# VectorE's loop of 267 instructions, and attention's probabilities signalled and turned token tile by token tile

## The chip, the cores and the metric

One core of a Trainium2 chip runs the whole program in one launch. The metric is the device time of that core in microseconds. The kernel before took 3623.44 us, the median of three runs (3611.81 to 3623.83).

## The reference, cut to what matters

The input is 64 blocks (graphs) of 256 tokens with 256 features, and for each block a 256 x 256 matrix `adj` of zeros and ones. All is float32. Four layers follow each other, each added to its input:

```
x = x + gnn0(layernorm(x), adj)     # graph attention: softmax over the edges, one head
x = x + mamba(layernorm(x))         # project, 4-tap causal convolution, silu, chunked state space, gate, project
x = x + gnn1(layernorm(x), adj)     # a weight matrix for each of 4 relations
x = x + moe(layernorm(x))           # 8 experts, one per token, capacity 1.25
```

The two parts that the change touches:

```
# the convolution, over time t, for each of 640 channels (5 blocks of 128)
conv[c, t] = conv_b[c] + sum(xBC[c, t - k] * conv_w[c, 3 - k] for k in range(4))
xBC = silu(conv)                    # 4 channel blocks are x, the fifth holds B and C
# the attention
e = where(adj > 0, leaky_relu(s1[:, None] + s2[None, :]), -9e15)
h = softmax(e, axis=-1) @ wh
```

## The kernel before, in words

A block's 256 tokens are two token tiles (T = 2) of 128 partitions. Each engine runs its own program, and the programs meet at semaphores only. The first three layers are a software pipeline: `step(b1, b2, b3, turn)` does the attention of block b1, the mamba layer of block b2 = b1 - 1 and the relations of block b3 = b2 - 1. `rounds` calls it: two opening steps and four more are written out, then comes a hardware loop (`eng.Fori`) of 28 iterations with two steps each, and then the closing steps. In the loop the count that a wait compares with is worked out by register instructions; in the unrolled steps it is a constant. Every second step (turn 0) holds `best_expert`, which picks each token's expert on VectorE, and `count` on TensorE; the other (turn 1) holds `slots`. Then 71 tiles of 256 tokens go through the experts; the change doesn't touch that part.

On VectorE a step is, in order: statistics of x (`deviation(0, ...)`, L828); `normalise(2, ...)` of x2 (L838); the taps of the convolution's block XB, which holds B and C; `remainder` (L909); the taps of the other four blocks; the chain of dt and the cumulative sums (L943 to L952); attention's leaky relu and masked maximum (L957, L962); xdt (L982); `slots` in turn 1; two products of the decay matrix with g (`weigh`, L855); with the sums of the exponentials done, x1 (L1007) and its statistics; two more products; y and its gating (L1023, L1028); row, the third residual (L1035); `best_expert` in turn 0; x2 (L1055) and its statistics; the logits lg (L1065).

Of the four taps ScalarE makes the first (`tap`, L628), and VectorE adds the other three in place (`taps`, L847). Each of these is followed by a wait of VectorE for its own instruction, since the next reads what it wrote. Three instructions of block XB, then three for each of the blocks 0 to 3: `conv_ready` goes up by 15 a step. TensorE waits for the third (it reuses bank 6 in L1289), ScalarE for the third and the fifteenth (the two silu).

In attention ScalarE makes the probabilities of each token tile (L726) and signals once after both. TensorE waits for that, turns the four 128 x 128 quarters into bank 0 (L1345), and signals; ScalarE copies them to `probT`, TensorE multiplies them with `wh` (L1370), and VectorE makes x1 from the result (L1007). When x1 is made, TensorE may fill banks 0 and 1 again with the next block's attention product (`attend`, L1181).

`need(eng, sem, n)` is a wait that is left out where n is a constant of zero or less. Many of them say that a buffer may be overwritten.

Of the kernel before, what the change touches and what calls it, by code (L numbers as in the profile page):

```python
# [5 lines left out]
ALU = mybir.AluOpType  # L6
ACT = mybir.ActivationFunctionType
# [13 lines left out]
def need(eng, sem, n):  # L21

    if isinstance(n, int) and n <= 0:
        return
    eng.wait_ge(sem, n)
# [24 lines left out]
def graph_mamba_moe(nc, io, out):  # L50
# [38 lines left out]
    with ctx:  # L89
# [531 lines left out]
        def _(act):  # L621
# [21 lines left out]
            def step(b1_, b2_, b3_, turn_):  # L643
# [51 lines left out]
                if b2_ is not None:  # L695
                    act.wait_ge(conv_ready, 15 * b2_ + 3)
                    need(act, g_made, b2_)
                    nc.scalar.activation(bT[:], conv[0:NS, XB, :], ACT.Silu)
                    nc.scalar.activation(cT[:], conv[NS:P, XB, :], ACT.Silu).then_inc(bc_ready, 1)
                    act.wait_ge(conv_ready, 15 * b2_ + 15)  # L700
                    need(act, yd_ready, 2 * b2_)
                    nc.scalar.activation(xs[:], conv[:, 0:XB, :], ACT.Silu).then_inc(xs_ready, 1)
                    act.wait_ge(proj_made, 5 * b2_ + 5)
                    nc.scalar.activation(zs[:, 2:4, :], bank[2][:, :], ACT.Silu).then_inc(zs_ready, 1)
# [17 lines left out]
                if b1_ is not None:  # L722
                    act.wait_ge(e_ready, b1_ + 1)
                    need(act, prob_turned, b1_)
                    for t in range(T):
                        ins = nc.scalar.activation(prob[:, t, :], e[:, t, :], ACT.Exp, bias=nmax[:, t:t + 1],  # L726
                                                   accum_out=esum[:, t:t + 1])
                    ins.then_inc(prob_ready, 1)
                    act.wait_ge(prob_turned, b1_ + 1)
                    need(act, hp_made, b1_)  # L730
                    copy(probT[:], bank[0][:, :]).then_inc(probT_ready, 1)
# [45 lines left out]
        def _(dve):  # L777
# [63 lines left out]

            def taps(c, b):

                src = bank[6][:, 0:N] if c == XB else bank[3 + c // 2][:, (c % 2) * N:(c % 2 + 1) * N]
                first = {XB: 0, 0: 3, 1: 6, 2: 9, 3: 12}[c]
                for k in range(1, TAPS):
                    v.scalar_tensor_tensor(conv[:, c, k:N], src[:, 0:N - k], conv_w[:, c, TAPS - 1 - k:TAPS - k],  # L847
                                           conv[:, c, k:N], ALU.mult, ALU.add).then_inc(conv_ready, 1)
                    dve.wait_ge(conv_ready, 15 * b + first + k)

# [60 lines left out]
            def step(b1_, b2_, b3_, turn_):  # L911
# [7 lines left out]
                if b2_ is not None:  # L919
                    if is_first(b2_):  # L920
                        dve.wait_ge(mix_in, 16 * len(mix_loads))
                    dve.wait_ge(tap_ready, 3 * b2_ + 1)
                    v.tensor_scalar(dt_pos[:], bank[6][:, N:2 * N], dt_b[:], 0.0, ALU.add, ALU.max)
                    taps(XB, b2_)
                if b3_ is not None:
                    remainder(b3_)
                if b2_ is not None:
                    for c in range(XB):
                        if c % 2 == 0:
                            dve.wait_ge(tap_ready, 3 * b2_ + 2 + c // 2)  # L930
                        taps(c, b2_)
                    if is_first(b2_):
                        dve.wait_ge(w_proj_made, 1)
                        for k in range(2):
                            ins = v.tensor_copy(w_proj[:, 2 * k:2 * k + 2, 0:D], bank[6 + k].rearrange("p (c d) -> p c d", d=D))
                        ins.then_inc(w_proj_ready, 1)
                        dve.wait_ge(a_exp, 1)
                        v.tensor_scalar(a_neg[:, 1:2], a_neg[:, 0:1], -1.0, None, ALU.mult).then_inc(a_ready, 1)
                        dve.wait_ge(a_ready, 1)

                    dve.wait_ge(dt_act, 3 * b2_ + 3)
                    need(dve, g_made, b2_)
                    ins = v.tensor_tensor(dt[:], dt_pos[:], dt_ln[:], ALU.add)  # L943
                    ins.then_inc(dt_ready, 1)
                    dve.wait_ge(dt_ready, b2_ + 1)
                    ch2.link(dve, v.tensor_scalar(dA[:], dt[:], a_neg[:, 1:2], None, ALU.mult), b2_)
                    ch2.link(dve, v.tensor_tensor_scan(cs[:], ones_row[:], dA[:], 0.0, ALU.mult, ALU.add), b2_)
                    ch2.link(dve, v.tensor_copy(cs_h[:], cs[:]), b2_)
                    ch2.link(dve, v.scalar_tensor_tensor(cs_r[:], cs_h[:], less_hi[:], cs[:], ALU.mult, ALU.add), b2_)
                    ch2.link(dve, v.tensor_copy(cs_m[:], cs_r[:]), b2_)  # L950
                    need(dve, expo_made, 8 * b2_)
                    v.scalar_tensor_tensor(cs3[:], cs_m[:], less_mid[:], cs_r[:], ALU.mult,  # L952
                                           ALU.add).then_inc(cs_ready, 1)
# [23 lines left out]
                if b2_ is not None:  # L977
                    dve.wait_ge(g_ready, b2_ + 1)
                    need(dve, y_made, 2 * b2_)
                    for t in range(T):  # L980
# [10 lines left out]
                if b1_ is not None:  # L991
                    dve.wait_ge(prob_ready, b1_ + 1)
                    ch1.link(dve, v.reciprocal(rsum[:], esum[:]), b1_)
# [20 lines left out]
                if b1_ is not None:  # L1014
                    need(dve, xn1_turned, b1_)
                    normalise(1, xn1, x1, xn1_ready, b1_)
                if b2_ is not None:
                    for u in range(2):
                        dve.wait_ge(y_made, 2 * b2_ + 1 + u)
                        if u == 0:  # L1020
                            need(dve, out_made, b2_)
                        for j in (2 * u, 2 * u + 1):
# [26 lines left out]
                if b2_ is not None:  # L1049
                    dve.wait_ge(rstd_ready[4], b2_ + 1)  # L1050
                    dve.wait_ge(x1b_ready, b2_ + 1)
                    if b3_ is not None:
                        dve.wait_ge(x2b_ready, b3_ + 1)
                    for t in range(T):
# [86 lines left out]
        def _(pe):  # L1141
# [90 lines left out]
            def step(b1_, b2_, b3_, turn_):  # L1232
# [36 lines left out]
                if b3_ is not None:  # L1269
                    if is_first(b3_):  # L1270
                        pe.wait_ge(rel_in, 16 * len(rel_loads))
                    if b2_ is not None:
                        pe.wait_ge(conv_ready, 15 * b2_ + 3)
                        pe.wait_ge(dt_act, 3 * b2_ + 1)
# [65 lines left out]
                if b1_ is not None:  # L1340
                    pe.wait_ge(prob_ready, b1_ + 1)
                    pe.wait_ge(wh_ready, b1_ + 1)
                    for k in range(T):
                        for t in range(T):
                            ins = turn(bank[0][:, k * N + t * P:k * N + (t + 1) * P], prob[:, t, k * P:(k + 1) * P],  # L1345
                                       identf[:])
                    ins.then_inc(prob_turned, 1)
# [163 lines left out]
```

## Time and profile before

| what | value |
|---|---|
| runs | 3623.83, 3611.81, 3623.44 us |
| the profiled execution | 3620.52 us |
| its span, first to last instruction | 3618.6 us |
| TensorE matmul busy | 3430.6 us (95%) |
| TensorE weight load busy | 2791.9 us (77%) |
| VectorE busy | 2565.8 us (71%) |
| GpSimd busy | 1784.1 us (49%) |
| ScalarE busy | 1734.8 us (48%) |
| mean granted TensorE clock | 0.981 |

The span is the time from the first to the last instruction of the execution that the profiler recorded. Register, branch, semaphore and DMA-issuing instructions don't count as busy. The pipelined steps take the first 2500 us or so of the span and the experts the rest; in the page's slices VectorE is busy for eight tenths and more in the former, and for four tenths in the latter.

### The profile page before, as it was taken

What the parts mean: (1) busy time and instruction counts of PE and PEld (TensorE: products, weight loads), DVE (VectorE), ACT (ScalarE), POOL (GpSimd) and SP (SyncE); (2) the same over time, 40 slices, a digit from 0 to 9 for tenths busy, and PEclk for the clock granted to TensorE, in tenths of its full rate; (3) what the DMA queues carried; (4) which work ended last, traced back from release to release, by engine and by line L of the source; (5) the groups of instructions that cost most, each with busy time, mean ns of one, the idle gap of its engine ahead of it and who ended that gap; (6) DMA issues with size and microseconds to landing.
All of it is one profiled execution on the core that took longest, in us unless ns stands there. A gap on an engine that the chain in (4) does not pass through costs nothing.

```text
span 3618.6 us, 63010 instructions
## 1 busy us (share of the span) xinstructions
PE 3430.6 (95%) x19338; PEld 2791.9 (77%) x19338; DVE 2565.8 (71%) x7349; ACT 1734.8 (48%) x3690; POOL 1784.1 (49%) x2043
## 2 busy tenths in 40 slices
PE   7999999999999999999999999999599999999998
PEld 6777777777777777777777777777488888888887
DVE  4888887888888788888888888888344444444444
ACT  3655655655555555565555566565133232232332
POOL 2455454554444455445555554555355455455553
PEclk8999999999999999999999999999799999999999
DMA  3111111111111111111111111110255555555553
GB/s 120 39 36 51 38 36 50 39 36 48 41 36 36 50 39 36 41 47 36 47 42 36 41 47 36 44 45 25 90 199 190 194 200 190 192 199 193 191 200 128
DMA packets 168301, 305.78 MB, mean 85 GB/s; under 512 B 38000, under 2 KB 140400, under 8 KB 149936
## 3 DMA queue, kind: packets, MB, share of 16 engines
q0 software_dynamic: 38272, 196.98, 15.7%
q1 hardware_dynamic: 92880, 72.41, 6.9%
q10 hardware_dynamic: 36960, 34.62, 3.3%
q14 instruction: 162, 1.33, 0.1%
q8 instruction: 27, 0.44, 0.1%
HBM read 250.77 MB, written 53.17 MB: 84 GB/s over the span
## 4 chain that ended last, share of the span: by engine, by line
PE 77%; DVE 12%; issue 6%; POOL 1%; ACT 1%; another core or an unknown queue 1%; DMA 0%; DVEq 0%; ACTq 0%; SPq 0%; POOLq 0%
PE bank L1444 13%; PE bank L1458 13%; PE bank L1188 9%; PE bank L1172 8%; PE bank L1403 6%; PE bank L1289 6%; PE bank L1388 5%; DVE conv L847 4%; PE bank L1181 3%; PE bank L1370 3%; PE bank L1320 1%; DVE decay L855 1%; DVE stats L828 1%; PE bank L1345 1%; PE bank L1216 1%
## 5 line engine op out<-in xcount | busy, mean ns | idle before, releaser
L768 ACT ACTIVATE decay<-bank,w_up 128x256 f32<-128x256 f32 x568 | 269.0, 474 | 700.8 <-PE bank L1444 693.0
L1172 PE MATMUL bank<-xn1T,w_in 128*128 128x256 f32 x2304 | 523.8, 381 | 5.7 <-issue 4.5
L1188 PE MATMUL bank<-w_rel,hT 128*128 128x264 f32 x2048 | 523.4, 394 | 0.0
L1444 PE MATMUL bank<-zs,w_up 128*128 128x256 f32 x2272 | 504.5, 380 | 0.6 <-ACT zs L623 0.6
L1458 PE MATMUL bank<-w_dn,decay 128*128 128x256 f32 x2272 | 502.1, 379 | 0.0
L847 DVE SCALAR_TENSOR_TENSOR conv<-bank,conv_w,conv 128x255 f32<-128x255 f32 (+2 forms) x960 | 461.4, 481 | 34.6
L1172 PEld LDWEIGHTS bank<-xn1T,w_in 128*128 128x128 f32 x2304 | 432.5, 190 | 64.5 <-issue 8.2
L1444 PEld LDWEIGHTS bank<-zs,w_up 128*128 128x128 f32 x2272 | 433.4, 191 | 60.3 <-issue 0.9
L1458 PEld LDWEIGHTS bank<-w_dn,decay 128*128 128x128 f32 x2272 | 426.2, 190 | 55.1
L1120 DVE TENSOR_TENSOR hT<-bank,w_dn 128x256 f32<-128x256 f32 x142 | 60.3, 425 | 536.8 <-PE bank L1458 536.8
L1188 PEld LDWEIGHTS bank<-w_rel,hT 128*128 128x128 f32 x2048 | 364.0, 190 | 79.3 <-issue 20.7
L482 POOL TENSOR_TENSOR rstd<-ve,mhalf 128x2 f32<-128x2 f32 x256 | 218.2, 853 | 389.3 <-DVE ve L833 344.3
L496 POOL TENSOR_SCALAR masks<-adjt_sb 128x512 fp32r<-128x512 int32 x256 | 404.3, 1592 | 5.4
L1289 PE MATMUL bank<-masks,xp 128*128 128x512 f32 x1024 | 287.9, 429 | 66.3 <-DVE conv L847 57.9
L855 DVE TENSOR_TENSOR decay<-decay,g 128x768 f32<-128x768 f32 x256 | 253.1, 1029 | 92.8 <-ACT decay L737 86.1
L361 POOL TENSOR_TENSOR beats<-mhalf 128x1 f32<-128x1 f32 x372 | 80.3, 216 | 462.6 <-DVE hT L1120 336.0
L1289 PEld LDWEIGHTS bank<-masks,xp 128*128 128x128 f32 x1024 | 197.4, 201 | 142.1 <-issue 67.9
L533 POOL TENSOR_TENSOR x2b<-x,b_rel 128x264 f32<-128x264 f32 x128 | 92.9, 746 | 417.1 <-DVE xdt L982 406.3
L737 ACT ACTIVATE decay<-bank 128x384 f32<-128x384 f32 x512 | 209.8, 496 | 124.0 <-PE bank L1226 90.3
L1403 PE MATMUL bank<-w_proj,y 128*128 128x264 f32 x1024 | 240.4, 387 | 3.1 <-DVE y L1028 3.0
L623 ACT ACTIVATE xn1T<-bank 128x512 f32<-128x512 f32 x64 | 38.2, 597 | 391.2 <-PE bank L1167 391.2
L1403 PEld LDWEIGHTS bank<-w_proj,y 128*128 128x128 f32 x1024 | 188.8, 190 | 35.5 <-DVE y L1028 6.5
(238 smaller groups left out, 6167.5 us busy)
## 6 DMA issues: line engine op xcount, KB each, us to landing
token_rows<-row SPq DMA_DIRECT2D x64, 266.0 KB, 2.9
xT_sb<-in_xT ACTq DMA_DIRECT2D x64, 256.0 KB
x_sb<-in_x ACTq DMA_DIRECT2D x64, 256.0 KB, 3.0
adj_sb<-in_adj SPq DMA_DIRECT2D x64, 256.0 KB, 3.2
adjt_sb<-in_adjT SPq DMA_DIRECT2D x64, 256.0 KB, 3.4
out<-row SPq DMA_DIRECT2D x64, 256.0 KB, 2.4
w_in<-token_rows,idc POOLq DMA_INDIRECT x142
out<-hT,ids POOLq DMA_INDIRECT x142
```

The lines of the kernel that those rows point to most:

```text
L482: gp.tensor_tensor(rstd[i][:], ve[i][:], mhalf[:], ALU.pow).then_inc(rstd_ready[i], 1)
L496: ins = gp.tensor_scalar(masks[:, :, r, :], adjt[:], float(r + 1), None, ALU.is_equal)
L737: nc.scalar.activation(decay[:, h, :], bank[EXPO[h % 4]][:, 0:TRI], ACT.Exp).then_inc(decay_ready, 1)
L768: nc.scalar.activation(hid(f), bank[f % 4][:, 0:GROUP], ACT.Relu, bias=b1[q % 2][:, f:f + 1]).then_inc(hid_ready, 1)
L847: v.scalar_tensor_tensor(conv[:, c, k:N], src[:, 0:N - k], conv_w[:, c, TAPS - 1 - k:TAPS - k], conv[:, c, k:N], ALU.mult, ALU.add).then_i ...
L855: v.tensor_tensor(decay[:, 2 * j:2 * j + 2, :], decay[:, 2 * j:2 * j + 2, :], g[:, 0:TRI].unsqueeze(1).broadcast_to([P, 2, TRI]), ALU.mult ...
L1172: ins = mm(dst, w_in[:, k, first:first + P], xn1T[:, k, :], start=k == 0, stop=k == DK - 1)
L1188: ins = mm(bank[6 + t][:, 0:GX], hT[:, d, r * N + t * P:r * N + (t + 1) * P], w_rel[:, r, d, :], start=r == 0 and d == 0, stop=r == R - 1 ...
L1289: ins = mm(bank[6 + c][:, :], xp[part][:, t, d * P:(d + 1) * P], masks[:, t, 2 * c:2 * c + 2, :], start=t == 0 and part == 0, stop=t == T ...
L1403: ins = mm(bank[(4, 2)[t]][:, 0:GX], y[:, j, t * P:(t + 1) * P], w_proj[:, j, :], start=j == 0, stop=j == XB - 1)
L1444: ins = mm(bank[f % 4][:, 0:GROUP], w1[i][:, k, f * P:(f + 1) * P], xgT[:, k, :], start=k == 0, stop=k == DK - 1)
L1458: ins = mm(bank[4 + j][:, 0:D], hid(f)[:, j * P:(j + 1) * P], w2[i][:, f, :], start=f == 0, stop=f == FB - 1)
```

## The change

`taps` takes a tuple of blocks. For each of the taps 1 to 3 it issues one instruction for each block of the tuple, and only the last of them signals and is waited for. It is called for (XB,), then for (0, 1) and for (2, 3), so `conv_ready` goes up by 9 a step; all that wait for it count by 9. Five `need` waits of VectorE are gone (for g_made, expo_made, y_made, xn1_turned and out_made), and before x2 so is the wait for x2b_ready, and the one for x1b_ready except in the last such step. ScalarE signals `prob_ready` after each token tile's probabilities. TensorE waits for tile 0, turns its two quarters, waits for tile 1, and turns its two; VectorE waits for both as before.

```diff
             # ScalarE
-                    act.wait_ge(conv_ready, 15 * b2_ + 3)
+                    act.wait_ge(conv_ready, 9 * b2_ + 3)
...
-                    act.wait_ge(conv_ready, 15 * b2_ + 15)
+                    act.wait_ge(conv_ready, 9 * b2_ + 9)
...
                     for t in range(T):
-                        ins = nc.scalar.activation(prob[:, t, :], e[:, t, :], ACT.Exp, bias=nmax[:, t:t + 1],
-                                                   accum_out=esum[:, t:t + 1])
-                    ins.then_inc(prob_ready, 1)
+                        nc.scalar.activation(prob[:, t, :], e[:, t, :], ACT.Exp, bias=nmax[:, t:t + 1],
+                                             accum_out=esum[:, t:t + 1]).then_inc(prob_ready, 1)
             # VectorE
-            def taps(c, b):
-
-                src = bank[6][:, 0:N] if c == XB else bank[3 + c // 2][:, (c % 2) * N:(c % 2 + 1) * N]
-                first = {XB: 0, 0: 3, 1: 6, 2: 9, 3: 12}[c]
+            def taps(blocks, b):
+
+                first = {XB: 0, 0: 3, 2: 6}[blocks[0]]
                 for k in range(1, TAPS):
-                    v.scalar_tensor_tensor(conv[:, c, k:N], src[:, 0:N - k], conv_w[:, c, TAPS - 1 - k:TAPS - k],
-                                           conv[:, c, k:N], ALU.mult, ALU.add).then_inc(conv_ready, 1)
-                    dve.wait_ge(conv_ready, 15 * b + first + k)
+                    for c in blocks:
+                        src = bank[6][:, 0:N] if c == XB else bank[3 + c // 2][:, (c % 2) * N:(c % 2 + 1) * N]
+                        ins = v.scalar_tensor_tensor(conv[:, c, k:N], src[:, 0:N - k], conv_w[:, c, TAPS - 1 - k:TAPS - k],
+                                                     conv[:, c, k:N], ALU.mult, ALU.add)
+                    ins.then_inc(conv_ready, 1)
+                    dve.wait_ge(conv_ready, 9 * b + first + k)
...
-                    taps(XB, b2_)
+                    taps((XB,), b2_)
...
-                    for c in range(XB):
-                        if c % 2 == 0:
-                            dve.wait_ge(tap_ready, 3 * b2_ + 2 + c // 2)
-                        taps(c, b2_)
+                    for u in range(2):
+                        dve.wait_ge(tap_ready, 3 * b2_ + 2 + u)
+                        taps((2 * u, 2 * u + 1), b2_)
...
-                    need(dve, g_made, b2_)
...
-                    need(dve, expo_made, 8 * b2_)
...
-                need(dve, y_made, 2 * b2_)
...
-                    dve.wait_ge(prob_ready, b1_ + 1)
+                    dve.wait_ge(prob_ready, 2 * b1_ + 2)
...
-                    need(dve, xn1_turned, b1_)
...
-                        if u == 0:
-                            need(dve, out_made, b2_)
...
-                    dve.wait_ge(x1b_ready, b2_ + 1)
-                    if b3_ is not None:
-                        dve.wait_ge(x2b_ready, b3_ + 1)
+                    if b1_ is None:
+                        dve.wait_ge(x1b_ready, b2_ + 1)
             # TensorE
-                        pe.wait_ge(conv_ready, 15 * b2_ + 3)
+                        pe.wait_ge(conv_ready, 9 * b2_ + 3)
...
-                    pe.wait_ge(prob_ready, b1_ + 1)
                     pe.wait_ge(wh_ready, b1_ + 1)
-                    for k in range(T):
-                        for t in range(T):
+                    for t in range(T):
+                        pe.wait_ge(prob_ready, 2 * b1_ + t + 1)
+                        for k in range(T):
                             ins = turn(bank[0][:, k * N + t * P:k * N + (t + 1) * P], prob[:, t, k * P:(k + 1) * P],
                                        identf[:])
                     ins.then_inc(prob_turned, 1)
```

The loop body of VectorE's compiled program has 300 instructions before the change, register, semaphore and branch instructions counted.

## Rows read from the trace of the kernel before

**Rows 1.** The page: busy time and instructions of each engine.
```profile
PE 3430.6 (95%) x19338; PEld 2791.9 (77%) x19338; DVE 2565.8 (71%) x7349; ACT 1734.8 (48%) x3690; POOL 1784.1 (49%) x2043
```
**Rows 2.** Windows, first two steps, then 53: length, busy (instructions), clock, DMA share, GB/s.
```profile
859.20:899.30 40.10, 37.25 (x229) 28.98 (x229) 31.21 (x90) 22.31 (x47) 21.63 (x23) 1.00 0.14 40
899.30:936.60 37.30, 36.67 (x226) 28.86 (x223) 34.01 (x103) 22.09 (x46) 18.23 (x20) 1.00 0.14 43
312.90:2390.20 2077.30, 1975.50 (x11928) 1549.79 (x11929) 1728.54 (x5030) 1178.12 (x2465) 1051.41 (x1141) 0.99 0.14 41
```
**Rows 3.** Waits, 312.9 to 2390.2 us: who waited for whom, us in total, times, longest.
```profile
PE bank L1289 <- DVE conv L847: 57.9, 27, 2.6
PE bank L1181 <- DVE x L1007: 15.8, 29, 3.0
PE bank L1345 <- ACT prob L726: 8.1, 15, 0.6
PE bank L1172 <- issue: 4.5, 24, 0.3
...
DVE stats L828 <- issue: 100.3, 27, 4.2
DVE x L1055 <- POOL rstd L482: 21.7, 27, 0.8
```
**Rows 4.** Timeline, step with the branch: start, us, engine line, ..., [idle before <- releaser].
```profile
862.06 0.36 DVE L1065 SCALAR_TENSOR_TENSOR lg<-row,gate_b 128x8 f32<-128x8 f32 x2
866.13 0.75 DVE L828 BATCH_NORM_STATS2 stats<-x_sb 128x6 f32<-128x256 f32 x2 [3.72 <-issue]
...
870.21 2.10 PE L1289 MATMUL bank<-masks,xp 128*128 128x512 f32 x8 [2.13 <-DVE conv L847]
...
883.02 0.66 PE L1345 MATMUL bank<-identf,prob 128*128 128x128 f32 x4 [0.50 <-ACT prob L726]
...
855.87 0.45 ACTq L646 DMA_DIRECT2D x_sb<-in_x  x1
```
**Rows 5.** Timeline of the other step, VectorE, TensorE and ScalarE.
```profile
907.54 6.25 DVE L847 SCALAR_TENSOR_TENSOR conv<-bank,conv_w,conv 128x255 f32<-128x255 f32 x12
...
922.54 2.28 DVE L855 TENSOR_TENSOR decay<-decay,g 128x768 f32<-128x768 f32 x2
...
924.92 0.89 DVE L1007 SCALAR_TENSOR_TENSOR x<-bank,rsum,x_sb 128x264 f32<-128x264 f32 x2
...
929.71 0.86 DVE L1023 SCALAR_TENSOR_TENSOR y<-xs,d_col,bank 128x256 f32<-128x256 f32 x2
...
925.96 2.09 PE L1181 MATMUL bank<-w_gc,xT_sb 128*128 128x274 f32 x8 [0.45 <-DVE x L1007]
...
921.60 1.64 ACT L737 ACTIVATE decay<-bank 128x384 f32<-128x384 f32 x4 [0.27 <-PE bank L1226]
```
**Rows 6.** The page's DMA queues: kind, packets, MB, share of 16 engines.
```profile
q14 instruction: 162, 1.33, 0.1%
```
**Rows 7.** The same of one iteration, 862.5 to 939.8 us.
```profile
q14 instruction: 5, 0.04, 0.2%
```
**Rows 8.** The same of 864.0 to 864.6 and of 933.0 to 933.8 us.
```profile
q14 instruction: 1, 0.01, 3.2%
...
q14 instruction: 1, 0.01, 4.0%
```
**Rows 9.** Windows of two unrolled or first-pass steps and of two long ones.
```profile
196.80:233.60 36.80, 36.42 (x227) 28.75 (x223) 33.84 (x102) 22.08 (x46) 18.04 (x20) 1.00 0.15 44
233.60:275.40 41.80, 38.20 (x230) 30.06 (x230) 31.07 (x91) 22.22 (x47) 21.40 (x24) 0.96 0.14 39
936.60:980.80 44.20, 39.48 (x229) 29.83 (x229) 31.48 (x92) 22.31 (x47) 21.10 (x23) 0.96 0.13 37
1097.20:1142.90 45.70, 39.99 (x229) 30.55 (x229) 31.28 (x91) 22.30 (x47) 22.03 (x23) 0.93 0.13 35
```
**Rows 10.** Timeline of ScalarE in the longest of them.
```profile
1128.48 1.64 ACT L737 ACTIVATE decay<-bank 128x384 f32<-128x384 f32 x4 [4.30 <-remote]
```

## The prediction

> **What bounds the kernel now.** The page's first part comes first: TensorE is busy for 95% of the span, VectorE for 71%, so TensorE sets the time, and only idle TensorE can be won [rows 1]. Next the windows by step. A step is the time from one block's first projection to the next block's. The hardware loop holds two steps: the first one after the branch back ("after-branch step") took 40.1 us, the second 37.3 us [rows 2]. In the former TensorE is busy 37.25 us, in the latter 36.67 us. The unrolled step at 196.8 us, of the same work as the latter, took 36.8 us [rows 9]. The window from 312.9 to 2390.2 us holds 27 after-branch steps and 26 others: 2077.3 - 26 x 37.3 = 1107.5 us, 41.0 us for each after-branch step.
>
> Then TensorE's waits in that window [rows 3]: 57.9 us for the depthwise convolution (L1289 behind VectorE's L847), 27 times, thus once an iteration; 15.8 us for x1 (L1181 behind L1007); 8.1 us for the probabilities (L1345 behind ScalarE's L726). VectorE's own largest is not a wait for anybody: 100.3 us of "issue", 27 times, at the first instruction after the branch. The timeline shows one: VectorE's last instruction starts at 862.06 and ends at 862.42, the next starts at 866.13, though its input was long there. TensorE is then 2.13 us late at L1289 and 0.50 us at L1345 [rows 4]. ScalarE's branch back costs nothing: its x_sb load is issued at 855.87, between two squares [rows 4]. In the other step VectorE has no gap up to x1, and TensorE waits 0.45 us for it at L1181 [rows 5].
>
> **Why the branch is slow.** The DMA queues name instruction transfers: q14, 162 packets in 1.33 MB, so 8.2 KB each [rows 6]. One iteration has five [rows 7], and single windows place them at 864.0-864.6, 866.5-867.1, 870.5-871.1, 901.5-902.2 and 933.0-933.8 us, one each ([rows 8] has the first and the last of the five). Compiled, VectorE's loop of the kernel before is 300 instructions, ScalarE's 180, TensorE's 957. Counting VectorE's instructions against these times: about 128 lie between the last three transfers. My reading: a block holds some 128 instructions, and entering a block fetches the next. The body begins 18 instructions (give or take 4) before the end of a block, so it lies in four blocks (18 + 128 + 128 + 26). Entering the fourth fetches a fifth, the first is gone, and the branch must fetch it (the packet inside the 3.72 us gap), then the second and third. ScalarE's 180 lie in two blocks by the same count, and none of the five transfers is left over for it. A buffer of two blocks would miss there and one of five would hit on VectorE, so it keeps three or four.
>
> **The change, part by part.**
> *The loop's length.* 267 instructions instead of 300. In three blocks (384) they fit if they begin at most 117 into a block. They begin 110 into one now, and the unrolled steps before the loop only lose instructions (waits on constants), so the start moves to between about 80 and 110. With four blocks kept, the first is still there at the branch: the 3.72 us go 27 times. VectorE's own gain is 100 us; TensorE's is read from its steps. Taking 2.13 and 0.50 out of 40.1 leaves 37.5 us [rows 2, 4]; TensorE is busy for 37.25 of them, and the rest is short waits for what the late VectorE made, so I take 37.3. The conv of the first block would be ready 3.7 us sooner, and TensorE needed it only 2.13 us sooner: 1.6 us of slack. From 41.0 to 37.3, 27 times: 100 us.
>
> This includes an irregular part. The two longest after-branch steps took 44.2 and 45.7 us with the clock granted at 0.96 and 0.93 [rows 9]; in the latter ScalarE's exponentials start 4.30 us late, put down to nobody [rows 10]. The first pass of the loop, with no branch before it, has such a step too (41.8 us, clock 0.96) [rows 9]. Beyond 40.1 us the two hold 4.1 + 5.6 = 9.7 us. The cause isn't visible. I let half go with the idle time and put back 5 us.
>
> *Taps by two blocks.* Each tap waits for the one before. Twelve such in a row took 6.25 us, (6.25 - 0.48) / 11 = 0.52 us from one start to the next; two independent ones of the same kind and size (L1023) take 0.86 us together, so the second starts 0.39 us after the first [rows 5]. Six pairs a step lose one dependence each: 6 x 0.13 = 0.8 us of VectorE per step. The removed waits were for things long done; between dependent instructions they show as short gaps, and I count 0.1 us. The other side of this bound: if a pair's second instruction gained nothing, 0; if every removed wait were a whole one, 1.2 us. I take 0.8, since L1023 is the same operation reading the same kind of bank.
> What lies on the path: in the other step x1 comes at 924.92 after two decay products that end at 924.82. They can't start before ScalarE's exponentials (921.60 plus 1.64, so 923.24), which leaves at most 923.24 + 0.95 + 0.15 = 924.3 for x1: 0.6 us to win [rows 5]. TensorE needs 0.45. The wait goes, with little to spare: 26 x 0.45 = 12 us in the window, and some 3 us in the seven steps before and behind it at up to the same 0.45. If VectorE gained nothing here, 0. What is late next is TensorE itself: VectorE's later idle time grows.
>
> *Convolution and silu.* ScalarE's silu of xs waits for the last tap as before, now 0.8 us sooner; it is off the path in the second step. The first blocks of a pair finish later than they did, but nobody waits for them singly.
>
> *Removed waits* (g_made, expo_made, y_made, xn1_turned, out_made, x2b_ready, x1b_ready): each is covered by a wait that stays, so nothing starts earlier by them; they count as loop length.
>
> *Probabilities by token tile.* TensorE turns tile 0 while ScalarE makes tile 1. One wait is added on TensorE, with the turn of tile 1 and everything after it behind it, and one register operation; such waits show as 4.5 us in 24 places at L1172 (0.19 us each) where TensorE has run dry, and as nothing under full queues [rows 3]. In the second step L1345 has no wait at all, so 0. In the after-branch step part of the 0.50 us, two turns of 0.66 / 4 = 0.16 us each, would go by this alone [rows 4]; with the stall gone it has no worth of its own. I bound it by -0.3 and +0.1 us a step, and take 0. VectorE waits for count 2b+2, the same moment as before.
>
> **The sum.** 3620.5 (the profiled execution, 1.9 us around a span of 3618.6) - 100 - 15 + 5 = 3510.5 us. That execution lies 2.9 us under the median of the runs, 3623.44, and 8.7 above the lowest. I forecast 3510 us.
> Its own range: the steps may keep 0.3 us of what I take out (56 x 0.3 = 17) or the pauses all stay (+8): 3535; all go and the register waits shrink too: 3494.
>
> **The rivals.**
> *The stall stays.* For: the trace shows only that a body in four blocks misses and one in two doesn't; 267 lies in three. If the buffer keeps three blocks, entering the third fetches the fourth and drops the first. Then 2.13 us remain, and the gain is the probabilities' 8.1 us, 12 + 3 us at L1181 and little else: 3620.5 - 23 = 3597 us. Against: four is the rounder size, and the count excludes only five and more. Chance 0.14.
> The Trainium skill ("Runtime: NRT & Kernel Launch", Instruction fetch mechanics) says the same in a stronger form: the buffer of an engine other than TensorE is two pages of 256 instructions, and a taken branch to a target outside them stalls. By that rule 267, more than a page, would still stall, and the time would be that 3597. The trace disagrees in the size: 8.2 KB packets in [rows 6], half of the page's 16 KiB; where it is right in the total of 512 instructions, it speaks for four blocks of 128.
> *Half of it.* The stall goes, but the after-branch step finds another limit at 38.5 us (best_expert adds VectorE work late in it, and TensorE's count waits for it): 27 x 1.2 = 32 us less gain, 3543 us. For: VectorE waits there 27 times, up to 0.8 us, for GpSimd's rstd before it can make x2 [rows 3], so the end of this step is a chain through three engines. Against: the same chain ends the step now, and TensorE's busy time of 37.25 us has no room for it [rows 2]. Chance 0.07.
> *Slower.* With fewer rests TensorE pauses more often, as in the 45.7 us step (5.6 us over the common one, clock 0.93 [rows 9]). From 110 / 5 = 22 more such pauses the gain is used up; at 27 the time is 3510 + 27 x 5 = 3645 us. For: one happened without a stall before it. Against: the second step, the denser one, takes 37.3 us each time. Chance 0.03.
>
> **Chances.** Forecast 0.76, stall stays 0.14, half 0.07, slower 0.03. The range that holds 8 in 10 has to reach the stall's case: 3494 to 3600 us; the likeliest case alone 3494 to 3535. About 0.5% (18 us) is what a measurement can tell from no change. Faster by more than that: 0.76 + 0.07, and of the stall's 0.14, as 3597 is only 0.6% below 3620, some 0.06: 0.89. Within 0.5%: 0.07. Slower: 0.04.
>
> **What would show it.** Right: VectorE's "issue" at L828 gone, q14 down from 162 packets to about 30, TensorE's waits at L1289 for L847 gone, both steps at 36.9 to 37.3 us, starts of paired taps 0.39 us apart. Wrong: 27 gaps of 3.7 us still there, steps of 40 us; or the wait at L1289 gone and a new one behind it.

## The result and the profile after

The changed kernel takes 3515.0 us, the median of four runs (3513.94 to 3518.75); the kernel before, on the same chip, 3621.56 us (3611.81 to 3623.83). The ratio is 0.971, with a 95% interval of 0.969 to 0.973. The forecast was 3510 us.

The page's first part, busy time and instructions of each engine, against [rows 1]: the engines run the same numbers of instructions, and TensorE is busy for 97% of a shorter span.
```profile
PE 3396.7 (97%) x19338; PEld 2783.3 (79%) x19338; DVE 2532.4 (72%) x7349; ACT 1723.9 (49%) x3690; POOL 1788.3 (51%) x2043
```
The instruction queue on the page, against [rows 6] (kind, packets, MB, share): five packets an iteration are gone.
```profile
q14 instruction: 27, 0.22, 0.0%
```
The same windows as in [rows 2] (first two steps of one iteration, then the 53 steps of the loop), and two long steps, which answer to [rows 9]. Columns: length, busy us of TensorE, its weight loads, VectorE, ScalarE and GpSimd, granted clock, DMA share, GB/s.
```profile
834.00:870.70 36.70, 36.63 (x228) 29.14 (x229) 30.62 (x89) 22.08 (x47) 21.52 (x23) 1.00 0.16 43
870.70:907.80 37.10, 36.47 (x228) 28.96 (x225) 33.58 (x103) 21.98 (x46) 18.25 (x20) 1.00 0.13 42
308.30:2285.20 1976.90, 1944.07 (x11928) 1542.89 (x11929) 1701.22 (x5029) 1167.79 (x2465) 1055.31 (x1141) 1.00 0.15 43
752.80:797.00 44.20, 39.31 (x229) 30.73 (x229) 30.63 (x89) 22.08 (x47) 21.08 (x23) 0.92 0.14 36
984.10:1025.10 41.00, 38.33 (x229) 30.03 (x229) 30.68 (x89) 22.08 (x47) 21.91 (x23) 0.96 0.15 39
```
The spans differ by 3618.6 - 3513.2 = 105.4 us. The loop's window has 2077.3 - 1976.9 = 100.4 of them, the steps before it 312.9 - 308.3 = 4.6, what follows it 0.4. The gain lies in the loop.

TensorE's waits in the loop's window, against [rows 3]:
```profile
PE bank L1174 <- DVE x L1004: 17.5, 31, 2.7
PE bank L1381 <- ACT decay L736: 7.5, 3, 4.8
PE bank L1165 <- issue: 5.9, 24, 0.3
```
The 57.9 us for the convolution have no successor at L1282 (L1289 before), and the 8.1 us for the probabilities none at L1338. The wait for x1 (L1174, before L1181) is still there: 17.5 us, where 15.8 were. VectorE's waits in the same window: 100.3 us of "issue" are gone, and nothing of its size has come.
```profile
DVE decay L856 <- ACT decay L736: 69.9, 28, 4.9
DVE xdt L979 <- ACT g L623: 39.9, 53, 1.0
DVE ve L1039 <- PE bank L1403: 38.3, 26, 1.5
...
DVE x L1048 <- POOL rstd L482: 21.7, 27, 0.8
```
VectorE's timeline at the branch, against [rows 4]: the first statistics of the next iteration start 0.42 us after the last instruction of the one before started. It was 4.07 us, 3.72 of them idle.
```profile
836.88 0.35 DVE L1058 SCALAR_TENSOR_TENSOR lg<-row,gate_b 128x8 f32<-128x8 f32 x2
837.30 0.75 DVE L827 BATCH_NORM_STATS2 stats<-x_sb 128x6 f32<-128x256 f32 x2
```
The timeline of the other step, against [rows 5] (ScalarE's g and exponentials, VectorE's three, TensorE's that waits, and GpSimd's masks, which will matter):
```profile
889.41 0.50 ACT L623 ACTIVATE g<-bank 128x400 f32<-128x400 f32 x1
...
889.95 1.29 DVE L979 TENSOR_TENSOR xdt<-bank,g 128x512 f32<-128x512 f32 x2 [0.50 <-ACT g L623]
...
892.78 1.64 ACT L736 ACTIVATE decay<-bank 128x384 f32<-128x384 f32 x4 [0.27 <-PE bank L1219]
...
893.05 4.41 POOL L496 TENSOR_SCALAR masks<-adjt_sb 128x512 fp32r<-128x512 int32 x3
...
893.68 2.26 DVE L856 TENSOR_TENSOR decay<-decay,g 128x768 f32<-128x768 f32 x2
...
896.05 0.89 DVE L1004 SCALAR_TENSOR_TENSOR x<-bank,rsum,x_sb 128x264 f32<-128x264 f32 x2
...
897.09 2.09 PE L1174 MATMUL bank<-w_gc,xT_sb 128*128 128x274 f32 x8 [0.40 <-DVE x L1004]
```
Read step by step over the whole loop (from one first projection to the next):

| | before | after | saved |
|---|---|---|---|
| after-branch step, median | 40.50 | 36.66 | |
| the same, mean of 27 | 41.00 | 37.52 | 3.48 x 27 = 94 us |
| other step, median | 37.30 | 37.09 | |
| the same, mean | 37.3 | 37.07 | 0.25 x 26 = 6 us |

The mean after the branch stands above the median because of seven long steps, such as the 44.2 and 41.0 us above: together they take 23 us more than common ones. With the first pass of the loop, which has one too (40.5 us, 41.8 before), it is eight and 27 us. I call such a step's excess over the median a pause; below, the pauses of a kernel are counted with the first pass, from 0.5 us of excess on.

Where the time of a pause goes can be read. In the 44.2 us step ScalarE stands before the second four of its exponentials, and TensorE then waits for them at L1381:
```profile
783.92 1.64 ACT L736 ACTIVATE decay<-bank 128x384 f32<-128x384 f32 x4 [7.40 <-remote]
785.69 5.39 PE L1381 MATMUL bank<-decay,xdt 128*64 128x256 f32 x32 [4.84 <-ACT decay L736]
```
In a common step the same ScalarE gap is 1.22 us (859.00) and the same 32 products take 2.82 us (862.05). TensorE's clock is granted at 1.2 GHz and not 2.4 from 784.3 us, when the engine had been idle since 780.9, to 791.1 us. So the step pays twice: 4.84 us of idle time and 2.57 us of slower products, of 7.5. In seven of the eight long steps ScalarE stands for 2.4 us or more before one of its two fours of exponentials. "remote" means that no instruction in the trace is the releaser: the products that ScalarE waits for end at 777.7, but their four semaphore updates are recorded at 783.90 to 784.00 us. In the common step they end at 858.97 and the updates stand at 858.98 to 859.08.

One number of the prediction has to be corrected first. Compiled, VectorE's loop body of the changed kernel is 279 instructions, not 267: the change's 267 leaves out 12 memsets that the count of 300 for the kernel before includes. The unrolled steps ahead of the loop lose 18. So by the prediction's own reading (blocks of 128, the body of the kernel before starting at place 110) the new body starts at 110 - 18 = 92 and ends at 92 + 279 = 371, still within three blocks (384).

### The profile page after: what moved, and what is told of

Its sections match the earlier page's. It is cut to its first block, busy times and chain, and to the rows that moved or that the text cites. A ratio compares the mean times of both kernels' runs of the same rounds, so it can differ in the third digit from the quotient of the medians.

```text
span 3513.2 us, 62394 instructions
## 1 busy us (share of the span) xinstructions
PE 3396.7 (97%) x19338; PEld 2783.3 (79%) x19338; DVE 2532.4 (72%) x7349; ACT 1723.9 (49%) x3690; POOL 1788.3 (51%) x2043
## 4 chain that ended last, share of the span: by engine, by line
PE 91%; issue 3%; DVE 3%; ACT 1%; POOL 1%; another core or an unknown queue 1%; DMA 1%; ACTq 0%; DVEq 0%; SPq 0%; POOLq 0%
PE bank L1165 14%; PE bank L1437 14%; PE bank L1451 14%; PE bank L1181 12%; PE bank L1282 7%; PE bank L1396 6%; PE bank L1381 5%; PE bank L1174 4%; PE bank L1363 3%; PE bank L1313 2%; PE bank L1235 2%; PE bank L1304 1%; DVE x L1004 1%; PE bank L1209 1%; PE bank L1403 1%
## 5 line engine op out<-in xcount | busy, mean ns | idle before, releaser
L1181 PE MATMUL bank<-w_rel,hT 128*128 128x264 f32 x2048 | 523.5, 394 | 0.0
L847 DVE SCALAR_TENSOR_TENSOR conv<-bank,conv_w,conv 128x255 f32<-128x255 f32 (+2 forms) x960 | 425.9, 477 | 20.8
L1181 PEld LDWEIGHTS bank<-w_rel,hT 128*128 128x128 f32 x2048 | 364.0, 190 | 80.0 <-issue 24.2
L856 DVE TENSOR_TENSOR decay<-decay,g 128x768 f32<-128x768 f32 x256 | 251.2, 1022 | 95.1 <-ACT decay L736 90.2
L1282 PE MATMUL bank<-masks,xp 128*128 128x512 f32 x1024 | 275.5, 413 | 5.7 <-ACT xp L623 5.6
L1282 PEld LDWEIGHTS bank<-masks,xp 128*128 128x128 f32 x1024 | 188.5, 189 | 68.6 <-ACT hT L623 25.7
```

The lines of the kernel that those rows point to most:

```text
L847: ins = v.scalar_tensor_tensor(conv[:, c, k:N], src[:, 0:N - k], conv_w[:, c, TAPS - 1 - k:TAPS - k], conv[:, c, k:N], ALU.mult, ALU.add)
L856: v.tensor_tensor(decay[:, 2 * j:2 * j + 2, :], decay[:, 2 * j:2 * j + 2, :], g[:, 0:TRI].unsqueeze(1).broadcast_to([P, 2, TRI]), ALU.mult ...
L1181: ins = mm(bank[6 + t][:, 0:GX], hT[:, d, r * N + t * P:r * N + (t + 1) * P], w_rel[:, r, d, :], start=r == 0 and d == 0, stop=r == R - 1 ...
L1282: ins = mm(bank[6 + c][:, :], xp[part][:, t, d * P:(d + 1) * P], masks[:, t, 2 * c:2 * c + 2, :], start=t == 0 and part == 0, stop=t == T ...
```

## The experiments

**Theory A** (the prediction's): the branch stalls when VectorE's body reaches into four blocks of some 128 instructions; position and length decide together. **Rival B**: the removed waits and pairs themselves made the loop fast. **Rival C**: only the body's length decides (300 too long, 279 not). The first four kernels tell them apart. They shift the body by cheap one-column memsets that run once, ahead of VectorE's first step:

**1. The kernel before, shifted by 30.**
```
+ spare = sb("spare", [P, 30])
+ for i in range(30):
+     v.memset(spare[:, i:i + 1], 0.0)
```
The body keeps its 300 instructions and all its waits; it starts at 110 + 30 - 128 = 12 and ends at 312.

> The kernel before, with nothing changed but 30 one-column memsets on VectorE ahead of its first step (some 2 us, beside the first loads). The loop body stays 300 instructions; its start moves from about the 110th place of a 128-instruction block to about the 12th, so it lies in three blocks (12 + 300 = 312, under 384) and not four. Theory A (position: the branch misses when the body touches four blocks): the 27 gaps of 3.7 us at L828 go, q14 falls from 162 packets to under 40, time about 3525 us, nearly all of the change's gain. Theory B (length: fewer instructions, or fewer waits, are what helped): the gaps stay, 3620 us.

Measured: 3541.66 us against 3633.77 of the kernel before beside it, ratio 0.975 (0.973 to 0.977). The page's instruction queue:
```profile
q14 instruction: 27, 0.22, 0.0%
```
Thirty added instructions, none in the loop, take (3633.77 - 3541.66) / 27 = 3.4 us off each iteration. B and C both fall: no wait was removed and the length is the same. Its steps are 36.77 and 37.30 us (medians), with thirteen long ones that hold 43.5 us. The time is 17 us over the expected 3525; the kernel before took 12 us more on this chip, too, than in the comparison above.

**2. The changed kernel, shifted by 30.** The same edit on the changed kernel: 279 instructions from place 122 to 401, in four blocks.

> The changed kernel with the same 30 memsets ahead of the first step. The body is the changed one (279 instructions in the compiled program), but starts near place 122, and 122 + 279 = 401 is over 384: four blocks. Theory A: the stall comes back whole, 27 gaps of 3.7 us, over 150 q14 packets, about 3600 us. Theory B: no gap, 3515 us plus at most 2.

Measured: 3666.54 us, ratio 1.009 (1.007 to 1.011): slower than the kernel before, with every part of the change in it. The page, then the waits of its loop, then VectorE at one branch:
```profile
q14 instruction: 162, 1.33, 0.1%
```
```profile
DVE stats L828 <- issue: 107.7, 27, 4.4
...
PE bank L1285 <- DVE conv L848: 96.6, 27, 4.0
...
DVE xn L838 <- issue: 30.5, 27, 1.3
```
```profile
1039.34 0.36 DVE L1059 SCALAR_TENSOR_TENSOR lg<-row,gate_b 128x8 f32<-128x8 f32 x2
1043.56 0.75 DVE L828 BATCH_NORM_STATS2 stats<-x_sb 128x6 f32<-128x256 f32 x2 [3.87 <-issue]
...
1045.91 0.73 DVE L838 TENSOR_SCALAR xn<-x,mv,rstd 128x256 f32<-128x256 f32 x2 [1.11 <-issue]
```
The stall is back, with the 162 packets, to the number those of [rows 6]. What the expectation of some 3600 us missed is the second gap: the body runs through a few instructions and enters the next block, whose transfer isn't there yet, and VectorE stands for another 1.11 us. Counted in the trace with register and semaphore instructions, nine instructions of the body come before this gap, not the 6 of place 122: the body starts at about 119. The kernel before then starts at 119 - 12 = 107, and the 21 instructions up to its block's end covered the transfer (it has no such gap). So TensorE waits 96.6 us for the convolution instead of 57.9. Its clock is granted at 0.96 or less in each of the 27 after-branch steps, and in about half of them in the kernel before (mean of the execution 0.973, against 0.981), which is part of why the step takes 41.95 us (median).

**3. The changed kernel, shifted by 60** (places 24 to 303), a control for the memsets.

> The changed kernel with 60 memsets ahead, the control for the one with 30: the body starts near place 24 of the next block, 24 + 279 = 303, three blocks again. Theory A: no gap, about 3515 us, though more memsets were added than in the slow one. If the memsets themselves cost something, over 3520 us here and less with 30.

Measured: 3525.88 us, ratio 0.971 (0.969 to 0.973), steps 36.67 and 37.09 us, 27 packets. The memsets cost nothing that shows; the place decides.

**4. The removed waits alone.** Taps one by one and probabilities as before:
```
- need(dve, g_made, b2_)
- need(dve, expo_made, 8 * b2_)
- need(dve, y_made, 2 * b2_)
- need(dve, xn1_turned, b1_)
- need(dve, out_made, b2_)
...
+ if b1_ is None:
      dve.wait_ge(x1b_ready, b2_ + 1)
```
291 instructions; the unrolled steps lose the same 18, so 92 to 383 by the prediction's count: one place short of the fourth block.

> The kernel before with only the seven waits of a step removed. Compiled, the body falls from 300 to 291 instructions and the unrolled part before it loses 18, so it starts near place 92 and ends at 383 of 384, with my uncertainty of 4 places. Theory A: either no stall at all (about 3525 us) or the whole stall (about 3618 us), nothing between. Theory B (gain in proportion to the instructions removed, 9 of 21): about 3575 us.

Measured: 3530.37 us, ratio 0.972 (0.970 to 0.974), steps 36.74 and 37.31 us.
```profile
q14 instruction: 27, 0.22, 0.0%
```
A few removed waits that nobody waited for give nearly the whole gain, by moving and shortening the code.

**5 and 6. The edge: shifted by 16 and by 8.** Places 108 to 387 and 100 to 379.

> The changed kernel with 16 memsets ahead of the first step: the body of 279 starts near place 108 and ends near 387, just over three blocks of 128. Theory A (three blocks fit, four don't, and the block's size is 128): the stall is back, over 150 q14 packets, 27 gaps at L828. If the capacity is something else (as a total of 400 or more), no stall.

> The same with 8 memsets: start near place 100, end near 379, inside three blocks. Theory A: no stall, under 40 q14 packets. Together with the run with 16 it places the edge between them, within the 4 places by which my start is uncertain.

Measured, one run each: 3511.58 and 3513.4 us, 27 packets in both. The shift by 8 is as expected. The one by 16 isn't: by my places it reached 3 into the fourth block. The second gap of experiment 2 says why. It puts every start some 3 places lower, which is within the 4 that the prediction allowed, and so this body at 105 to 384, just inside three blocks. The packets agree: in experiment 2 the last three of an iteration start when VectorE has begun the 15th, 138th and 262nd instruction of its body, in the kernel before the 26th, 150th and 281st, in all 27 iterations to within one. Moved by 18 - 16 = 2 places, the last would stand at the 283rd, and this body has 279. That a block holds some 128 instructions rests on these distances (123 to 131) and on the 8.2 KB packets [rows 7, 8]; it is not measured to the instruction. One rival is hardly touched by the shifts: that only the place of the start decides, whatever the length. It would need its limit between this start and that of the kernel before, 2 places higher.

**7 and 8. The other two parts, each alone, with the stall out of the way** (both on the shifted kernel of experiment 1). Taps by two blocks (`for c in blocks:` inside the tap loop, one signal for each pair), and the probabilities tile by tile:
```
- for k in range(T):
-     for t in range(T):
+ for t in range(T):
+     pe.wait_ge(prob_ready, 2 * b1_ + t + 1)
+     for k in range(T):
```


> The kernel before with its loop shifted by 30 memsets (no stall) and the taps paired, nothing else. Without the pairing the common steps took 36.77 us after the branch and 37.30 us for the second; in the changed kernel 36.66 and 37.09. If the pairing is what separates them: 36.7 and 37.1 here. If it is the removed waits or the split of the probabilities: 36.77 and 37.30.

> The kernel before with its loop shifted by 30 memsets (no stall) and the probabilities signalled and turned tile by tile, nothing else. My forecast was 0 for this part once the stall is gone: 36.8 and 37.3 us, as without it. Rival: the added wait costs up to 0.1 us a step, or the earlier turn of tile 0 gains up to 0.3 us a step.

Measured, one run each: 3502.57 us with the taps, steps 36.77 and 37.06 us; 3518.42 us with the probabilities, steps 36.67 and 37.37 us. Against 36.77 and 37.30 of experiment 1, pairing gives 0.24 us in the other step and nothing after the branch, so 28 x 0.24 = 7 us; the probabilities -0.10 and +0.07, nothing. The totals mislead here: the first is 39 us under experiment 1, but its pauses hold 9.7 us where the other's held 43.5, a difference of 34. The two also ran on different chips, on which the kernel before took 3615.74 and 3633.77 us. I don't take 3502.57 for a faster version: by its common steps it is the changed kernel (36.66 and 37.09).

**9. What holds up x1.** In the changed kernel VectorE waits 0.50 us for g (889.41, behind ScalarE's load of the table for Exp). Theory G: g ahead of that load brings x1 earlier by up to 0.4 us. Rival: the exponentials and probabilities then come later by as much.
```
- nc.scalar.preload_act_table(ACT.Exp)
  (the copy of g)
+ nc.scalar.preload_act_table(ACT.Exp)
```


> The changed kernel, with ScalarE's copy of g moved ahead of the load of the exponential's table (one statement moved, same instructions). In the changed kernel VectorE waits 0.5 to 1.0 us in each step at xdt (L979) for g, 46.8 us in all, and TensorE still waits 0.40 us for x1 at L1174 in each second step. Theory G (VectorE's gain from the paired taps is lost in this wait): xdt starts about 0.5 us sooner, the 0.40 us at L1174 go, second steps fall from 37.09 to about 36.7 us, time down by about 28 x 0.4 = 11 us or 0.3% against the changed kernel (ratio to before about 0.968). Rival: ScalarE's probabilities come 0.5 us later and TensorE waits at its turn of them instead: no gain or a loss of a few us.

Measured: 3536.93 us, ratio 0.979 (0.977 to 0.980), so slower than the changed kernel (0.971) by 0.8%, more than the few us of the rival; steps 37.43 and 37.38 us. Windows of two steps, the two waits of the whole execution that grew, and the timeline behind the exponentials:
```profile
842.40:879.90 37.50, 36.92 (x229) 29.09 (x229) 31.16 (x90) 22.19 (x47) 21.88 (x23) 1.00 0.15 43
879.90:917.30 37.40, 36.66 (x227) 28.84 (x224) 33.58 (x103) 22.09 (x46) 18.96 (x20) 1.00 0.14 42
```
```profile
PE bank L1174 <- DVE x L1004: 28.2, 59, 2.4
DVE decay L856 <- ACT decay L736: 133.5, 65, 4.0
```
```profile
901.65 5.11 POOL L496 TENSOR_SCALAR masks<-adjt_sb 128x512 fp32r<-128x512 int32 x3
...
903.12 2.29 DVE L856 TENSOR_TENSOR decay<-decay,g 128x768 f32<-128x768 f32 x2 [0.78 <-ACT decay L736]
```
G falls. VectorE's wait moved from g to the exponentials (133.5 us in place of 90.2 in the whole execution of the changed kernel), and TensorE now waits for x1 in both steps (59 times in place of 40, 28.2 us in place of 22.1). The idle time before xdt was not the limit; the exponentials behind it were.

**10. Where the pauses come from.** They fall in steps of the after-branch kind alone (the first of an iteration's two), which also hold GpSimd's scatter of slot numbers, four indirect DMAs that it issues 12.1 to 16.1 us into the step. Theory P: the scatter makes them. Theory Q: something else of that step. The edit moves the scatter to the end of the other step (`to_place` returns `turn_[0] - 1` in turn 1).

> The changed kernel, with GpSimd's scatter of slot numbers (four indirect DMAs for each group) moved from the first kind of step (after the branch) to the end of the second kind. The irregular pauses of 1 to 8 us lie in the first kind alone, in every run so far (27 us in all in the changed kernel). Theory P (the scatter makes them): they move into second steps, or go. Theory Q (something else of the first kind, as best_expert, or the loop's iteration): they stay in the first kind, in about the same iterations (profile steps 5, 19, 23 to 31).

Measured: 3641.82 us, ratio 1.007 (1.006 to 1.009); steps 41.50 and 37.05 us. The waits of its loop:
```profile
DVE x L1047 <- POOL rstd L482: 156.6, 27, 5.8
```
```profile
PE bank L1164 <- DVE x L1047: 81.8, 27, 3.1
```
The scatter stands ahead of the rstd that x2 needs, and the whole of it comes onto the path: a wait of 0.8 us at most in the changed kernel is 5.8 here. Four steps are still long (42.7 to 43.4 us, 6.3 us of excess in all, where 17 to 27 were), and they are after-branch steps. But the scatter hasn't left these: it runs across the start of the step, here one that starts at 785.3 us.
```profile
784.71 1.09 POOL L489 DMA_INDIRECT slot_ids<-tid,slot  x1 [0.15 <-issue]
786.11 0.97 POOL L489 DMA_INDIRECT slot_ids<-tid,slot  x1 [0.31 <-issue]
```
The pauses' own gap is gone: in the loop's window ScalarE has no wait of "remote" at its exponentials, where the changed kernel had 24.1 us in six. What is left of that kind is earlier in the step, as the scatter is, and short:
```profile
ACT z L708 <- remote: 1.9, 1, 1.9
ACT hT L622 <- remote: 1.7, 1, 1.7
```
So the place and size of the pauses changed with the scatter's place, which speaks for P. It isn't shown: the new wait of 5.8 us leaves the rest of the step more room, and the other edit that would tell, a kernel without the scatter, wasn't run.

**11. The slow product.** The second of the two decay products takes 1.38 us where the first takes 0.96 (893.68 and 894.56 in the changed kernel). One of GpSimd's masks starts at 894.53. In the kernel of experiment 9 it is the first product, at 903.12, that takes 1.42 us, and there a mask starts at 903.13. One more one-column product on GpSimd ahead of the masks should shift them against VectorE's.
```
+ carry(pool)
  edge_masks(0, R - 1)
```


> The changed kernel with one more one-column product on GpSimd (0.19 us) ahead of its edge masks in each step. In every run so far the second decay product of the second kind of step takes 1.38 to 1.41 us where the others take 0.95 us; it starts 0.03 us after GpSimd has begun its second mask. In the first kind it starts before the first mask ends, takes 0.95 us, and the mask takes 2.2 us and not 1.5. Theory C (the two engines take turns, and the later one waits, so that 0.15 us of order decide 0.43 us of VectorE): with the masks 0.19 us later the product takes 0.95 us in both kinds, the mask 2.2 us, TensorE's 0.40 us at L1174 go, second steps 37.09 -> 36.7 us, and the time falls by 28 x 0.4 = 11 us against after_again. Rival D (the 1.38 us come from what the product reads or from ScalarE): products and steps as before, 0 us.

Measured: 3513.28 us, ratio 0.970 (0.969 to 0.972), steps 36.76 and 37.25 us.
```profile
899.03 4.40 POOL L496 TENSOR_SCALAR masks<-adjt_sb 128x512 fp32r<-128x512 int32 x3
...
899.65 2.28 DVE L857 TENSOR_TENSOR decay<-decay,g 128x768 f32<-128x768 f32 x2
```
The products begin 0.62 us behind the masks here and 0.63 us in the changed kernel (893.05 and 893.68): both moved together, so the order that I wanted to change stayed, and the second product still takes 1.41 us. The experiment missed its aim. Over the whole of the changed kernel, 29 of the 256 products start within 0.05 us of a mask's start, and all 29 take 1.37 to 1.39 us; the first product above, which starts 0.63 us into a mask, takes 0.96. That the common start is the cause is argued, not shown.

**12. The changed kernel again, without an edit,** to see how much pauses vary.

> The changed kernel, unchanged: its ratio on this chip, for comparison with after_beat, and a second profile of it. The irregular pauses: if they belong to the loop's iterations (the data or the program), the same profile steps are long as before (5, 13, 19, 23, 25, 27, 29, 37); if they are chance, other ones are.

Measured: 3510.5 us, ratio 0.970 (0.969 to 0.972), steps 36.68 and 37.08 us. Counted from the kernel's first step as 0, so that the loop's window begins with step 7, its long steps are 5, 13, 19, 25, 27 and 29, and they hold 17 us. In the first profile it was the same six with 23 and 37 (11 just passes 0.5 us), and 27 us. Step 5 is long in all other kernels but that of experiment 10, step 19 in all but the one with the taps of experiment 7; the other numbers come and go. So pauses are no pure chance: some iterations have them nearly always, and their sum varies by ten microseconds and more between executions. Over all kernels here they held 6 to 43 us of a profile. Differences between kernels under some 20 us must be read from the common steps, not from one total.

## Why the prediction was right

**The stall.** Right in mechanism, shown by experiments 1 to 4 in both directions: it can be taken out of the unchanged loop and put into the changed one by its place alone. The reading of the packets (five an iteration, blocks of some 128, four kept) gave both signs. The rule of the Trainium skill ("Runtime: NRT & Kernel Launch", Instruction fetch mechanics) that I weighed as a rival is two pages of 256 instructions and a stall for a target outside them. What these runs exclude is my reading of it, by which any body longer than a page stalls: 300 instructions in a row are taken back without a stall in experiment 1, and 279 stall in experiment 2. The stalls alone don't exclude its page size: of all kernels here, the two that touch four blocks of 128 are also the only ones that would touch three pages of 256, if such pages ended at places 128 and 384. What speaks for 128 is the packets, 8.2 KB each and some 128 instructions apart. The rule's total of 512 instructions agrees with four blocks of 128.

**The count of 267** was wrong (279), and the conclusion held since 371 is still under 384. Had the unrolled steps not lost 18 instructions, it would not have held: 110 + 279 = 389. The prediction should have tried both counts.

**The size of the after-branch step.** Predicted 37.3 us, measured 36.66: 27 x 0.64 = 17 us more than forecast. The step at fault was taking TensorE's busy 37.25 us [rows 2] for a floor: in the same step it is busy 36.63 us now, with the same products. Part of the difference is how busy time adds up. In the changed kernel the first mask product starts at 842.60 us, 0.35 us before the projection's last one ends (835.88 + 7.07 = 842.95), and the two overlap; in the kernel before the projection ended at 868.08 and TensorE stood still, with nothing to overlap. So a wait that goes takes some busy time with it.

**The pauses.** I put back 5 us; the window has 23 in seven steps: 18 us less gain. They need no stall before them. That half of them would go with the idle time was a guess, and a wrong one. I called the cause not visible; the row that I had shows the place at least, since its 4.30 us [rows 10] are the same ScalarE gap as the 7.40 us above. The wrong guess cancels the error before it: 94 us saved after the branch where 95 were forecast. So the forecast's closeness here is partly luck.

**Pairing and x1.** Each pair did gain: the starts of the taps from 991.83 to 993.13 us lie 0.40, 0.50 and 0.40 apart, thus 0.90 us for a pair and a dependence where two single taps took 1.03, 0.8 us in six pairs, as forecast. What failed is the ceiling behind it. I allowed 0.95 us for what follows the exponentials to x1; the second product takes 1.38, and the row that I worked from had it (two products in 2.28 us, so 1.14 each on average [rows 5]). With it, x1 at 923.24 + 1.38 + 0.15 = 924.77 leaves 0.15 us to win and not 0.6. Measured, x1 comes 25.62 - 25.35 = 0.27 us sooner in its step. The wait went from 0.45 to 0.40 us, not to zero. The step still gained 0.21 to 0.24 us, so 6 us with a few outside the loop, where 15 were forecast.

**The probabilities.** Predicted nothing within -0.3 and +0.1 us a step; measured -0.10 and +0.07, in one run.

**The sum** with the measured terms: 3620.5 - 27 x (41.00 - 36.66) + 23 (pauses) - 6 (other step) - 5 (outside the window) = 3515 us, which is the profiled execution's time; it must be, since its terms are taken from that profile. The rivals "stall stays" and "half" are excluded by the 27 packets and by 36.66 us; "slower" had a true part, since pauses without a stall are there, but it needed 110 us of them, and 23 are there.

**Open:** why the semaphore updates that ScalarE waits for come up to 6.2 us late, whether the scatter does it, and why some iterations have it nearly always; the edge of a block to the instruction; whether the mask's start lengthens the product.

## What to carry to other kernels

Where an engine's first instruction after a loop's branch waits for "issue" and the instruction queue moves packets every iteration, count the loop's compiled instructions and where they start in their blocks: moving the loop, by a few instructions ahead of it, can be worth more than shortening it, and an edit that does nothing else can lose it again. When two versions are compared, compare common steps first and count the long ones apart; a total mixes them. Before earlier work is credited with time, follow the chain behind it to its next input, with the duration that an operation has in that place, not its shortest.

## What the runs showed of the hardware

VectorE's instruction fetch here moves 8.2 KB a packet, and a body that reaches into four blocks of some 128 instructions costs 3.7 to 3.9 us at each branch, while one of the same length in three costs nothing that shows. A body that started some nine instructions before a block's end paid a second time, 1.11 us; one that started some 21 before it did not. The same VectorE product took 0.95 us, or 1.37 to 1.42 us when a GpSimd instruction began at the same moment. TensorE's semaphore updates were recorded up to 6.2 us behind the end of the products that make them, in steps that mostly recur in the same iterations; in one of the longest the clock was granted at 1.2 GHz for 6.8 us behind it, and the same 32 products took 5.39 us instead of 2.82.
